# Two attention stages of one kernel: a unit's 18 input transfers paced over its slots, and in the causal attention the turn of the second half's maxima one slot earlier and the last output two slots later

## What is computed

```
def _L0_attn_ref(x, ...):                      # B, L, D = 2, 1024, 128; 16 heads of 8, 4 key/value heads
    scores = jnp.einsum('bhqd,bhkd->bhqk', q, k) / jnp.sqrt(jnp.float32(hd))
    attn = jax.nn.softmax(scores, axis=-1)
    attn = jnp.einsum('bhqk,bhkd->bhqd', attn, v)
    ...
def _reference_tuple_inner(x, W_dq, ...):      # second attention: 16 heads of 8, causal
    attn = jnp.einsum('bhtl,bsl->bhts', q_lat, c_kv) / math.sqrt(hs)
    attn = jnp.where(causal_mask[None, None], -jnp.inf, attn)
    attn = jax.nn.softmax(attn, axis=-1)
    ...
x = x + _L0_attn_ref(_layernorm(x, axis=-1), ...)
x = x + _L0_ffn_ref(_layernorm(x, axis=-1), ...)
x = x + _L1_attn_ref(_layernorm(x, axis=-1), ...)
x = x + _L1_ffn_ref(_layernorm(x, axis=-1), ...)
```

## Time and profile before

| | us |
|---|---|
| three timed runs, median | 1929.22 |
| lowest, highest | 1924.08, 1932.25 |
| profiled execution, its time | 1937.3 |
| profiled execution, its span | 1935.5 |
| PE busy | 1639.5 (85%) |
| DVE busy | 1480.4 (76%) |
| ACT busy | 1351.8 (70%) |
| POOL busy | 888.8 (46%) |
| mean granted PE clock | 0.918 of full |

### The profile page before, as it was taken

The page is one execution under the profiler, slowest core; times in us unless marked ns, Lnnn a source line. Parts: engine busy times, 40 slices in busy tenths (PEclk is TensorE's granted clock), DMA queues, the critical chain, the costliest instruction groups (busy, mean ns, idle before and its releaser), DMA issues. The chain is left out here.

```text
span 1935.5 us, 45994 instructions
## 1 busy us (share of the span) xinstructions
PE 1639.5 (85%) x17410; PEld 875.8 (45%) x17422; DVE 1480.4 (76%) x1729; ACT 1351.8 (70%) x2673; POOL 888.8 (46%) x572
## 2 busy tenths in 40 slices
PE   6789999999787776777677779989998998999996
PEld 2235555555344443444344433435555555344442
DVE  3588999999299999999999955457787835456456
ACT  4417888888799999999999943425676773654443
POOL 1066666665199999999999960000000002000000
PEclk9758999999988889898888889978999998999998
DMA  2344444443588988888988930202131100000000
GB/s 116 122 158 142 157 157 159 159 155 127 180 320 302 317 306 309 301 291 300 313 301 306 308 128 1 65 19 60 28 53 28 29 4 17 1 1 0 0 6 17
DMA packets 82504, 278.86 MB, mean 144 GB/s; under 512 B 11159, under 2 KB 11954, under 8 KB 81311
## 3 DMA queue, kind: packets, MB, share of 16 engines
q1 hardware_dynamic: 68223, 225.67, 35.2%
q0 software_dynamic: 13824, 50.34, 6.6%
q10 hardware_dynamic: 288, 0.45, 0.1%
HBM read 214.72 MB, written 61.21 MB: 143 GB/s over the span
## 5 line engine op out<-in xcount | busy, mean ns | idle before, releaser
L1645 POOL TENSOR_TENSOR hc<-st,ct 128x1024 f32<-128x1024 f32 x256 | 598.0, 2372 | 5.0 <-DVE st L1604 4.7
L1604 DVE TENSOR_TENSOR_SCAN st<-da,banks 128x1024 f32<-128x1024 f32 x256 | 562.3, 2265 | 14.5 <-ACT da L1561 5.9
L509 ACT ACTIVATE attn_probs<-banks 128x512 f32<-128x512 f32 (+3 forms) x640 | 325.5, 535 | 111.7 <-PE banks L345 94.6
L345 PE MATMUL banks<-attn_qa,attn_ka 75*32 75x512 bf16 (+3 forms) x3584 | 352.1, 366 | 17.5 <-DMA attn_qa<-attn_mrow 9.8
L562 DVE TENSOR_REDUCE attn_mx<-banks 128x1 f32<-128x1024 f32 x256 | 309.8, 1223 | 31.6 <-PE banks L345 19.4
L345 PE MATMUL banks<-attn_ka,attn_qa 72*32 72x512 bf16 (+3 forms) x3584 | 294.4, 382 | 23.9 <-DVE attn_mx L559 12.1
L1569 ACT ACTIVATE ut<-b_turned,mats 128x128 f32<-128x128 f32 x1024 | 311.6, 387 | 1.7
L1561 ACT ACTIVATE da<-dt,mats 128x1024 f32<-128x1024 f32 x256 | 282.3, 1138 | 24.3 <-DVE st L1604 16.2
L1486 PE MATMUL banks<-hc,onecol 128*32 128x512 f32 x1024 | 158.3, 694 | 106.6 <-POOL onecol L1643 83.0
L559 DVE CUSTOM_DVE_ANT_0 banks<-banks,attn_maskwide 128x128 f32<-128x128 f32 (+7 forms) x256 | 191.8, 775 | 49.1 <-PE banks L345 44.5
L740 POOL TENSOR_TENSOR made_ahead<-b_turned,x_turned 128x1024 f32<-128x1024 f32 x96 | 183.9, 1915 | 91.5 <-DVE attn_mparts L576 66.4
(11 more groups left out here) (445 smaller groups left out, 1963.0 us busy)
## 6 DMA issues: line engine op xcount, KB each, us to landing
dt<-dt_rows SPq DMA_DIRECT2D x256, 512.0 KB, 5.7
ahead<-made_ahead POOLq DMA_DIRECT2D x96, 512.0 KB, 3.6
ua<-ahead SPq DMA_DIRECT2D x96, 512.0 KB, 6.0
attn_qa<-q_lin SPq DMA_DIRECT2D x144, 64.0 KB
attn_ka<-k_lin SPq DMA_DIRECT2D x72, 64.0 KB
moe_w<-in_moe_w SPq DMA_DIRECT2D x2, 2048.0 KB, 10.0
mats<-in_mats SPq DMA_DIRECT2D x1, 2988.5 KB, 13.1
xparts_kept<-xparts_lin SPq DMA_DIRECT2D x3, 512.0 KB, 4.6
```

The source lines that it names most:

```text
L345: last = nc.tensor.matmul(out[sl(t, 32), :], lhs[:, sl(t, 32)], rhs, start=start, stop=True, skip_group_check=True)
L509: nc.scalar.activation(probs[s % 4][:, jj, c0:BLK], scores_exp[jj][:, c0:BLK], ACT.Exp, scale=scale).then_inc(probs_ready, 1)
L1604: nc.vector.tensor_tensor_scan(st[n % 4][:, :], da[n % 4][:, :], pair[:, :, :].rearrange("p h t -> p (h t)"), 0.0, ALU.mult, ALU.add).then ...
L1645: nc.gpsimd.tensor_tensor(hc[n % 8][:, :], st[n % 4][:, :], ct[:, b * SEQ:(b + 1) * SEQ], ALU.mult)\
```

## The change

1. **Pace.** Each of the 18 transfers of a unit i of at least 2 waits until a given slot of unit i-2 has been reached (`exp_scored`). In the first attention they are spread over slots 13 to 18, 19 to 22 and 23 to 26; in the second over 5 to 10, 14 to 17 and 18 to 21. This replaces the one wait for the ring buffer.
2. **SP's order**, second attention only: the rows of half 0 of unit i+1 go out between the first part of the loads and the other two.
3. **Second half's maxima** are turned in slot 3 and not 4, ahead of the output of the unit before, which goes from slot 3 to 5. The waits on bank 7 follow: this turn waits for the norm before last and for the copy of half 0; the output waits for the copy of half 1.
4. **Filler** of unit 0 goes from slots 1 to 4 and 7 to 10 to slots 1 to 3 and 6 to 10.

```
+        turn_at = [done_half[0] + 2, done_half[1] + 2]
+        OUT_AT = 5 if causal else 3
+        LOAD_SLOT = [5, 14, 18] if causal else [13, 19, 23]
+        LOAD_SPAN = [6, 4, 4]
...
+                def pace(i, p, n):
+                    if i >= 2:
+                        slot = LOAD_SLOT[p] + n * LOAD_SPAN[p] // 6
+                        sp.wait_ge(exp_scored, 2 * (NE * (i - 2) + slot))
...
-                    elif p == 0:
-                        sp.wait_ge(exp_scored, 2 * NE * (i - RING + 1))
...
                     for j in range(9):
                         if K_ORDER[j] == p:
+                            pace(i, p, done)
+                            done += 1
                             load_k(sp, i, j)
                         if Q_ORDER[j] == p:
+                            pace(i, p, done)
+                            done += 1
...
                 for i in range(UNITS):
                     rows(i, 1)
                     if i + 2 < UNITS:
-                        load(i + 2)
-                    if i + 1 < UNITS:
+                        load_part(i + 2, 0)
+                    if causal and i + 1 < UNITS:
+                        rows(i + 1, 0)
+                    if i + 2 < UNITS:
+                        load_part(i + 2, 1)
+                        load_part(i + 2, 2)
+                    if not causal and i + 1 < UNITS:
                         rows(i + 1, 0)
...
# turn_max
-                        pe.wait_ge(normed, 2 * i - 1 + half)
+                        pe.wait_ge(normed, 2 * i - 1 + (half if not causal else 0))
+                    if causal and half == 1:
+                        pe.wait_ge(mrow_ready[0], i + 1)
# turn_out
-                        pe.wait_ge(mrow_ready[0], i + 2)
+                        pe.wait_ge(mrow_ready[1 if causal else 0], i + 2)
# body, on PE and on DVE
-                        if s == 3 and i > 0:
+                        if s == OUT_AT and i > 0:
```

More of the change, by code:

```diff
@@ L228, in attention @@
         done_half = [slot_of((1, first_half - 1)), slot_of((0, NM - 1))]
-        turn_at = [done_half[0] + 2, max(done_half[1] + 2, 4)]
+        turn_at = [done_half[0] + 2, done_half[1] + 2]
+        OUT_AT = 5 if causal else 3
+        LOAD_SLOT = [5, 14, 18] if causal else [13, 19, 23]
+        LOAD_SPAN = [6, 4, 4]
         loaded = [k.sem(f"{tag}_loaded{i}") for i in range(2)]
@@ L278, in load_part @@
                             .then_inc(ones_in[i], 16)
-                    elif p == 0:
-                        sp.wait_ge(exp_scored, 2 * NE * (i - RING + 1))
                     if i >= 2 and p == 0:
                         sp.wait_ge(loaded[i % 2], 18 * 16 * (i // 2))
+                    done = 0
                     for j in range(9):
                         if K_ORDER[j] == p:
+                            pace(i, p, done)
+                            done += 1
                             load_k(sp, i, j)
                         if Q_ORDER[j] == p:
+                            pace(i, p, done)
+                            done += 1
                             sp.dma_start(qa[i % RING][HD * j:HD * j + HD, :, :],
@@ L437, in body @@
                         odd = s % 2 == 1
-                        if causal and i == 0 and s in (1, 2, 3, 4, 7, 8, 9, 10):
-                            pe.wait_ge(mrow_ready[0 if s < 7 else 1], 1)
+                        if causal and i == 0 and s in (1, 2, 3, 6, 7, 8, 9, 10):
+                            pe.wait_ge(mrow_ready[0 if s < 6 else 1], 1)
                             filler(turned[:, :])
```

## The result

| | before | changed | ratio, 95% interval |
|---|---|---|---|
| first measurement, median | 1930.74 | 1907.92 | 0.9877 [0.9838, 0.9917] |
| repetition | 1935.45 | 1906.29 | 0.9866 [0.9841, 0.9891] |

The change takes 22.8 us off by the medians; in the repetition, beside another group of runs of the kernel before, 29.2 by the medians and 25.9 by the ratio. The forecast was 1917, 12 under the kernel before, with a range down to 1911, so the measured 1907.9 lies outside it: the forecast had the sign and both mechanisms, and too little of each. The profiled execution of the changed kernel took 1912.95, with a span of 1911.1.

What follows compares the result with a forecast made beforehand. PE was taken to set the pace in the second attention. From the median, 1929.2 - 9.6 (PE's waits) + 0.6 (ACT's copy) - 3.2 (stalls) gave 1917, range 1911 to 1925.

Steps and rivals of the forecast that it cites:

- What bounds the kernel: Second attention: PE sets the pace, busy 32.53 of 35 us; its waits for maxima rows, DVE's norm and "issue" cost time.
- The turn in slot 3: Second attention, all units: earlier maxima remove PE's waits for their rows (6.9) and DVE's norm (2.7), 9.6 us in all.
- The 0.6 for ACT's copy: Second attention: ACT's copy of the maxima, ahead of slot 4's exponentials, delays them; 0 to 2.4 us in all, taken as 0.6.
- The pace: Second attention: spreading the 18 loads removes PE's "issue" stalls and their wake, 3.2 us in the median run, bounds 0 and 9.2.
- the bound of 9.2: Second attention: upper bound for stalls and wake removed by spreading loads, 7.2 + 2.0 us, as in the profiled execution.
- The forecast's other sum: Whole kernel, against the profiled execution of 1937.3 instead of the median: all 9.2 us of stalls and wake go, giving 1919.1.
- What holds the instructions up: Second attention: PE's instructions come by DMA and wait behind the backlog of loads; stalls of 1.77 and 5.39 us.
- The rival by the Trainium skill's: Second attention: a fetch waits for a packet, not the backlog, so the stalls stay; 1920, chance 0.20.
- Hardly a backlog: Second attention, slots 14 to 21: 12 paced loads take 11.2 us in 11.0 us of slots, so the stalls are gone.
- The low clock at 1372 to 1376: Second attention: a 3.2 us stretch at granted clock 0.50 behind waits of slots 4 and 8; its removal not counted on.
- First attention: First attention: its loads were already spread by their own length, so pacing them has effect 0, bounds -1 and +1.
- Loads late: Second attention: paced last loads land too late for the next unit's slot 2, PE waits in six units; 1941, chance 0.04.

Runs made afterwards that it cites:

- the turn alone: Kernel before with only the second half's maxima turned in slot 3, the output in slot 5 and the filler to match: 1918.89 against 1931.34, ratio 0.9936.
- the later run: Changed kernel with unit 4's 18 loads in one run from slot 10, in the second attention: 1905.8, ratio 0.9871 to the kernel before.
- the run put back: Changed kernel with unit 4's 18 loads in one run from slot 5, in the second attention: 1915.75 against 1929.78 for the kernel before, ratio 0.992.
- the single transfer: Changed kernel with the three transfers of the rows of maxima made one: 1901.22, ratio 0.9873 to the kernel before.

## Why the prediction was wrong, point by point

**What bounds the kernel: right.** PE set the pace, its three waits were the ones to go, and no other engine became the bound.

**The turn in slot 3: right in its mechanism, too small.** The sum said -9.6 + 0.6 = -9.0, or 1.1 a unit. A regular unit fell by 1.49. From PE's waits over one regular unit (1411.02 to 1444.05 before, 1404.58 to 1436.10 after):

```profile
PE banks L345 <- DMA attn_qa<-attn_mrow: 0.9, 1, 0.9
PE banks L345 <- DVE attn_mx L559: 0.7, 3, 0.3
PE banks L369 <- DVE ssm_in L589: 0.4, 1, 0.4
```

```profile
PE banks L362 <- DVE attn_mx L578: 0.5, 2, 0.3
```

The 0.9 and the 0.4 went, as summed. Besides them the wait of 0.18 for DVE's maxima in slot 3 went, which fits the four matmuls of the turn that now stand ahead of it, and PE's busy time fell from 30.53 to 30.40. The 0.6 for ACT's copy didn't come: the exponentials follow it at once and PE waits for nothing new. Six units give 8.9. The last unit, which before has a further wait of 1.07 for its rows and 0.52 for the norm, took 44.5, 44.9 and 45.7 us from its copy to the end in the three traces with the old turn. Behind those waits the granted clock fell in all three, to 0.50 to 0.69 over 4 us. With the new turn it took 42.0 in ten of twelve traces, at the full clock, and 43.6 and 43.7 in the turn alone and in the later run, at 0.66 to 0.68. So it gives 1 to 3.7, most often 2.5 to 3. Together that is some 10 to 12.5, beside the 12.4 measured for the turn alone. Unit 0 can't be read so: its stretch is longer or shorter with how long the clock stays at 0.50 in it, in kernels of every kind. The term of 9.0 took only what a wait list names and put a price on the only new cost it saw.

**The pace: the step that failed.** "The profiled execution is 8.1 above the median, so the median has about 12.4 - 8.1 = 4.3 of irregular time". This took the whole difference between two executions as a difference in this one stage. It wasn't. In the second execution of before, which took 1930.31, near the median, the stage has 11.3 us over against 12.2. The stalls belong to the program, at the same instruction, and not to a bad execution. The term was 3.2 and measured 9.9; the bound of 9.2 was the right value. The stated range missed for both reasons: its lower end of 1911 has the whole 9.2 in it, but nothing for a turn that gives more than 9.0. With the measured 12.4 in its place it would be 1929.2 - 12.4 - 9.2 = 1907.6, beside the measured 1907.9. The forecast's other sum, against the profiled execution, 1937.3 - 9.6 + 0.6 - 9.2 = 1919.1, would have given a change of -18.2. The trace spoke for that sum: both long intervals, the whole 12.4 us, had a stall in them, and both stalls stood behind a run of loads.

**What holds the instructions up: right in kind.** "PE's instructions come by DMA too and were held up behind the backlog." The queue of kind instruction shows it, and the run put back brings the stall with 8.6 us. The Trainium skill, "Runtime: NRT & Kernel Launch", section Instruction fetch mechanics, has blocks of 16 KiB fetched over a queue of the engine's own. The trace agrees with the size (124 packets, 2.03 MB), and with the queue as far as it has some of kind instruction that carry nothing else. The page also has a cost mostly hidden, which holds for the first attention and for four of the six runs of 18 (no issue stall), and not for those in unit 0 (0.9 to 2.0 us) and unit 4 (5.1 to 5.7 us). The rival by the Trainium skill's "DMA: Bandwidth & Descriptors", section Queues, rings and completion order, turns between queues packet by packet, isn't borne out in unit 4: one instruction packet starts 8.6 us behind the start of a run of nine loads and 15.1 behind that of a run of 18, where single turns would make no difference between the two.

**"Hardly a backlog": half right.** The 12 loads behind slot 14 are still a short run, and three traces have a stall of 1.0 to 1.6 behind it, a fourth one of 0.5.

**The low clock at 1372 to 1376, "I don't count on it": right.** The second trace of before has the same waits in slots 4 and 8 and no such stretch: the granted clock is 1.00 from 1350 to 1470, and the 2.3 us over in this unit are its stall of 1.99. It belonged to one execution, and cost it 3.2 us. That the stage took as long in the other (293.5 and 293.8 us) is in part chance: there the second stall and its wake were 1.5 us longer.

**First attention: right, nothing.** From ACT's first copy of the kind above to its last there are 320.0 and 320.2 us before, 319.7 and 319.7 in the changed kernel. SP's order and the filler never ran by themselves, and no trace shows a cost of either. Loads late: no wait for a load in any trace with 18 a unit. Of the signs in "what would show it" two came otherwise: the unit took 31.53 and not 31.8, and the DMA share near 0.5 over most of slots 5 to 21 wasn't there. By windows of 4 us in unit 4 it is 0.31 to 0.35 behind slot 5, 0.00 at 1466 to 1470, where the pace has its gap, and 0.30 to 0.55 behind slot 14.

**What stays open.** When a block of instructions is asked for isn't in the trace; that it joins a line at that moment is what fits unit 4 with runs of 9, 18 and 24 loads, not a thing seen. Why the packets of units 1, 2, 3 and 5 get through a run of 18, at 6 to 9 us, and why some executions of the run in unit 4 escape isn't known.

## What to carry to other kernels

Don't turn the difference between a profiled execution and the median into a correction for the stage that you look at: find in the trace where the excess lies, and take an "issue" stall that stands behind the same run of transfers as part of the program until a second trace says otherwise. Where an engine runs straight-line code, look at the DMA view's instruction packets beside the runs of loads: at one place in the program nine loads (8.4 us) in one go cost nothing and 18 cost 8.6 us with the clock's fall, at four others 18 cost nothing, and spreading the same loads costs nothing anywhere. In a chain that one wait closes, making it shorter can give more than the waits that are named: the turn gave 1.49 a unit for 1.1 summed, the single transfer 4.4 us for 2.8.

## What the runs showed of the hardware

A 16 KB instruction packet took 0.9 to 1.4 us alone and up to 1.75 beside loads, and PE went on 1.5 to 2 us behind its end (1484.3 to 1486.28 before, 1474.4 to 1475.96 in the run put back). Counted from the first load of a run, the next packet in unit 4 (next to the one that comes within 0.2 us before to 2 us behind this load) started after 8.6 us with 9 loads, after 14.1 to 15.1 with 18 and after 15.4 with 24. In units 1, 2, 3 and 5 of the kernel before it started after 6.2 to 8.8 us with 18. The loads keep only 8 to 9 of the 16 DMA engines busy (share 0.54). A stall of 5.3 us cost 3.3 more through the granted clock, which stood at 0.50 from 1476 to 1480 when PE came back, and at 0.70 over the 4 us behind.
